# State sums moved from TensorE and PSUM to columns and accumulating DMAs, with one up and gate part issued ahead

## What is computed

```python
    x = x + jnp.tanh(g_xattn[0]) * _L0_xattn_ref(ctx_1024, _layernorm(x, axis=-1), ...)
    x = x + jnp.tanh(g_ffn[0]) * _L0_ffn_ref(_layernorm(x, axis=-1), ...)
    return x
```

```python
            def step(state, xs):
                d_t, B_t, C_t, u_t = xs
                dA = jnp.exp(d_t[..., None] * A)
                state = state * dA + (d_t * u_t)[..., None] * B_t[:, None, :]
                y_t = jnp.einsum('ben,bn->be', state, C_t)
                return (state, y_t)
            ...
            y = y + D[None, :, None] * u
            y = y * jax.nn.silu(z)
```

```python
        def _expert_ffn(x, w1, wg, w2):
            return jax.nn.silu(x @ w1) * (x @ wg) @ w2
        output = _expert_ffn(x, Ws1, Wsg, Ws2)
        ...
        for e in range(NUM_ROUTED):
            w_e = jnp.sum(topk_probas * (topk_idxs == e), axis=-1)
            output = output + _expert_ffn(x, W1[e], Wg[e], W2[e]) * w_e[..., None]
```

## Time and profile before

| | us |
|---|---|
| median of 3 runs | 1498.68 |
| lowest and highest | 1497.59, 1501.57 |
| the profiled execution | 1496.58 |
| its span, first to last instruction | 1494.5 |
| mean granted TensorE clock | 0.968 of full |
| PE busy | 1397.6 (94%) |
| DVE busy | 1053.1 (70%) |
| ACT busy | 510.0 (34%) |
| POOL busy | 453.6 (30%) |

### The profile page before, as it was taken

One profiled execution on the slowest core, in us unless ns is written; L12 is line 12 of the kernel. 1 busy time (PEld: TensorE's weight loads), 2 busy tenths in 40 slices (PEclk: granted clock), 3 DMA queues, 4 the chain that ended last, 5 costly groups with the idle time before them and its releaser, 6 DMA issues.

```text
span 1494.5 us, 18163 instructions
## 1 busy us (share of the span) xinstructions
PE 1397.6 (94%) x6311; PEld 1078.6 (72%) x6311; DVE 1053.1 (70%) x1259; ACT 510.0 (34%) x855; POOL 453.6 (30%) x240
## 2 busy tenths in 40 slices
PE   8599869999999989999999979999999999999999
PEld 4244456877777776787787867787778878888887
DVE  5898855899998974588999874689999853222222
ACT  3676625544444323432322223432332211111111
POOL 3200004687777721123323211122332211111111
PEclk9599989999999999999999999999999999999999
DMA  6111634567765574455555564455555554655552
GB/s 206 43 64 57 252 121 171 204 248 272 243 244 206 212 249 141 143 192 179 177 173 181 174 247 128 143 184 179 185 176 172 184 191 156 210 194 191 189 168 84
DMA packets 90796, 266.36 MB, mean 178 GB/s; under 512 B 11472, under 2 KB 11600, under 8 KB 90336
## 3 DMA queue, kind: packets, MB, share of 16 engines
q1 hardware_dynamic: 85472, 258.39, 51.0%
q10 hardware_dynamic: 5248, 6.96, 1.3%
HBM read 207.39 MB, written 57.93 MB: 178 GB/s over the span
## 4 chain that ended last, share of the span: by engine, by line
PE 68%; DVE 18%; issue 6%; ACT 5%; DMA 2%; SPq 1%; POOL 0%; ACTq 0%; DVEq 0%; POOLq 0%
PE ps_hg L461 19%; PE ps_h L461 18%; PE ps_y L461 12%; PE ps_y L612 7%; DVE st L1098 7%; PE ps_mid L538 5%; DVE y_rows L1104 3%; ACT dA L791 2%; PE ps_h L530 2%; DVE st L1089 1%; DVE u L1000 1%; PE ps_mid L508 1%; DVE h_tmp L1224 1%; PE ps_mid L501 1%; DVE h_tmp L1219 1%
## 5 line engine op out<-in xcount | busy, mean ns | idle before, releaser
L1363 POOL TENSOR_TENSOR h_lo<-h_tmp,h_hi 128x512 fp32r<-128x512 f32 x128 | 280.8, 2194 | 781.7 <-ACT h_hi L863 781.7
L461 PE MATMUL ps_h<-x_hi,w_split 128*128 128x512 f32 x1024 | 350.8, 404 | 9.0 <-issue 4.6
L461 PE MATMUL ps_hg<-x_hi,wg_split 128*128 128x512 f32 x1024 | 349.8, 403 | 3.4 <-DVE h_tmp L1224 3.4
L1098 DVE TENSOR_TENSOR_SCAN st<-dA,st 128x1024 f32<-128x1024 f32 x128 | 298.5, 2341 | 0.0
L461 PE MATMUL ps_y<-w_split,h_hi 128*128 128x512 f32 x1024 | 258.2, 400 | 0.8 <-ACT h_hi L863 0.8
L461 PEld LDWEIGHTS ps_h<-x_hi,w_split 128*128 128x128 f32 x1024 | 195.1, 191 | 50.8 <-issue 6.9
L863 ACT ACTIVATE h_hi<-h_tmp 128x512 fp32r<-128x512 f32 x128 | 81.0, 632 | 430.6 <-DVE h_tmp L1224 430.6
L461 PEld LDWEIGHTS ps_hg<-x_hi,wg_split 128*128 128x128 f32 x1024 | 195.3, 191 | 44.4 <-issue 4.2
L461 PEld LDWEIGHTS ps_y<-w_split,h_hi 128*128 128x128 f32 x1024 | 190.3, 190 | 40.0 <-ACT h_hi L863 2.0
L1219 DVE SCALAR_TENSOR_TENSOR h_tmp<-h_tmp,ps_h 128x512 f32<-128x512 f32 x128 | 87.8, 686 | 182.8 <-ACT h_tmp L857 182.4
L461 PE MATMUL ps_hg<-x_lo,wg_split 128*128 128x512 f32 x512 | 202.1, 395 | 0.0
(11 more groups left out here) (140 smaller groups left out, 1133.5 us busy)
## 6 DMA issues: line engine op xcount, KB each, us to landing
w_split<-split_scratch SPq DMA_DIRECT2D x192, 512.0 KB, 4.9
wg_split<-split_scratch SPq DMA_DIRECT2D x96, 512.0 KB, 4.2
split_scratch<-w_split SPq DMA_DIRECT2D x64, 512.0 KB, 4.3
b_all<-xd_scratch SPq DMA_DIRECT2D x64, 256.0 KB, 4.0
split_scratch<-wg_split SPq DMA_DIRECT2D x32, 512.0 KB, 3.1
w_raw<-in_W_dram SPq DMA_DIRECT2D x14, 1024.0 KB, 7.6
wg_raw<-in_Wg_dram SPq DMA_DIRECT2D x7, 1024.0 KB, 10.0
dA<-in_x_dram SPq DMA_DIRECT2D x4, 1024.0 KB, 11.0
```

Of the source, the lines that this page charges most:

```text
L461: mm = pe.matmul(out_, lhs[a], rhs[c], start=first and q == 0, stop=last and q == len(sides) - 1)
L1098: dve.tensor_tensor_scan(flat[1], flat[0], flat[1], 0.0, ALU.mult, ALU.add).then_inc(scan_done, 1)
L1363: pool.tensor_tensor(h_lo[:, j, :], h_tmp[j % 2][:], h_hi[:, j, :].bitcast(F32), ALU.subtract).then_inc(hl_ready, 1)
```

## The change

For batches 1 to 3 (batch 0's block alone at the start keeps its sums on TensorE):

- The state is not transposed. VectorE multiplies the scanned state by the broadcast C row in one 128x2048 instruction (`cmul`), and GpSimd issues a DMA that adds the 1 MB tile to `yacc` in SBUF (`sum_state`, which waits for `cmul` and for the previous such DMA). The last state is added by VectorE (`last_add`). The B broadcast becomes a B and C broadcast of 512 KB into `ctxT` and `in_w`, which are free by then.
- `slot` is now one quarter each of `bmul` (both halves), scan, scan, `cmul`. `bmul` of state n waits until the DMA of state n - 2 has landed, since it writes the same `st` tile.
- The `init` and `z` and `ccols` work leaves TensorE: D times u is a ScalarE copy in columns, z stays in columns. After `make_y` four groups of transposes (`y_to_rows`) bring y to rows once, and `residual` reads them from PSUM.
- `ps_hg` has two banks and `ps_y` two. TensorE's step runs up(1), gate(1) ... gate(3), then up(0) and gate(0) of the next step, then the four down tiles one at a time. VectorE, ScalarE and GpSimd follow that order.
- GpSimd's loop over the experts of batches 1 and 2 is written out.

```diff
@@ TensorE
-            def step_(step, between=lambda g: None, before_down=None):
-
+            def step_(step, ahead=True, between=lambda g: None):
+
-                for j in range(T):
+                for j in range(1, T):
                     up(step, j)
...
                     gate(step, j)
...
+                if ahead:
+                    up(step + 1, 0)
+                between(2 * T - 2)
+                if ahead:
+                    gate(step + 1, 0)
+                between(2 * T - 1)
+                for i in range(T):
+                    down(step, i)
+                    between(2 * T + i)
...
-                        front(m, *{5: ("xproj", "init0"), 6: ("dt0", "init1"), 7: ("dt1", "ccols"), 8: ("dt2", "init2"),
-                                   9: ("dt3", "init3"), 10: ("z0", "z1")}.get(g, ()))
+                        front(m, *{3: ("xproj",), 4: ("dt0",), 5: ("dt1",), 6: ("dt2",), 7: ("dt3",)}.get(g, ()))
...
-                for e in range(2, NE):
-                    step_(STEPS * b + e, state_sums(m, 3 * (e - 2)))
-                step_(STEPS * b + NE, state_sums(m, DS - 1))
+                for e in range(1, NE):
+                    step_(STEPS * b + e)
+                step_(STEPS * b + NE, False, lambda g: y_to_rows(m) if g == 5 else None)
@@ VectorE
-            def sum_rows(m, n, i):
-
-                bank, before = mid(m, sum_place(m, n, i))
-                dve.wait_ge(mid_done[bank], before + 1)
-                dve.scalar_tensor_tensor(out=y_rows[:, i, :], in0=ps_mid[bank][:], scalar=c_cols[:, i, n:n + 1],
-                                         in1=y_rows[:, i, :], op0=ALU.mult, op1=ALU.add).then_inc(mid_read[bank], 1)
+            def cmul(m, n):
+
+                odd = n % 2
+                dve.wait_ge(scan_done, 2 * (DS * m + n + 1))
+                dve.tensor_tensor(st[odd][:], st[odd][:], bc_pair[odd][:, 1:2, :].broadcast_to([P, T, L]),
+                                  ALU.mult).then_inc(cmul_done, 1)
@@ VectorE, bmul
+                    if some(m) and n >= 2:
+                        dve.wait_ge(ysum_st, sums_before(m, n - 1))
@@ GpSimd
+            def sum_state(m, n):
+
+                pool.wait_ge(cmul_done, DS * (m - 1) + n + 1)
+                if n == 0:
+                    pool.wait_ge(yinit_done, T * m)
+                if some(sums_before(m, n)):
+                    pool.wait_ge(ysum_st, sums_before(m, n))
+                pool.dma_start(yacc[:], st[n % 2][:], accum_op=ALU.add).then_inc(ysum_st, 16)
...
+                for e in range(2, NE):
+                    n = 3 * (e - 2) + 1
+                    sum_state(m, n - 1)
+                    step_(STEPS * b + e, True, lambda j: sum_state(m, n + j - 2) if j > 1 else None)
@@ ScalarE, the decays of a sum step
-                    routed_step(STEPS * b + e, lambda j: decays(m, ahead + 3 * j, ahead + 3 * (j + 1)))
+                    def some_decays(j):
+                        first = T * (3 * (e - 2) + 2) + 3 * (j - 1)
+                        decays(m, first, first + 3)
+
+                    step_(STEPS * b + e, True, lambda j: some_decays(j) if j == T else None, some_decays)
@@ SyncE
+                    sp.wait_ge(cmul_done, DS * (m - 1) + n - RING + 1)
+                src = xd_dram[m].rearrange("(c n) l -> n c l", c=2)[bass.ds(n, 1)].broadcast_to([P, 2, L])
+                sp.dma_start(bc_pair[n % RING][:], src).then_inc(bc_ld[n % RING], 16)
```

480 lines of the change are left out of this document (268 added, 212 removed).

## The result

The changed kernel takes **1520.88 us** (median of 4 runs, 1519.52 to 1523.09) against 1498.13 for the kernel before (4 runs, 1495.32 to 1501.57): a ratio of 1.0152, 95% interval [1.0127, 1.0178]. It is slower by 1.5%, where I forecast 1482; inside the range of 1452 to 1550, with the sign wrong.

A forecast was written before the change was run, and what follows sets the result against it. VectorE's work plus waits was to bound batches 1 and 2, its exclusion with GpSimd batch 0. -18 + 19.5 - 21.3 + 3 = -16.8 took 1496.58 to 1479.8, stated as 1482 us; range 1452 to 1550, the forecast's own 1466 to 1494 (0.45).

The forecast's parts named there:

- VectorE's work and waits, 38.1 a step: Sum steps of batches 1 and 2: VectorE's work of 34.1 plus waits makes 38.1 us, against 39.9; -18 in all.
- waits of 0.7, 1.9 and 1.4: VectorE, batches 1 and 2: 0.7 for up(1)'s tanh, 1.9 behind GpSimd's `h_lo`, 1.4 for a decay ahead of a tanh.
- TensorE's 32.64 hides in it, with or without the part ahead: Sum steps of batches 1 and 2: TensorE's 32.64 us of matmuls fit within VectorE's 38.1, adding nothing.
- Both at nothing while DMAs land in time.: GpSimd and SyncE queues: waits behind accumulating DMAs and fetches behind the B and C load cost nothing if DMAs land in time.
- the closest call: Accumulating DMA: taken as hidden in about 12.5 us before the waiting `bmul`; a plain 1 MB DMA lands in 11.0.
- rival 1: DMA engines bound the sum steps, an accumulate costing twice a copy: +68 us, 1550; chance 0.25.
- Rival 2: Only one accumulate's latency is too long, 12 us and 1.2 to issue: +27 us, 1509; chance 0.16.
- Batch 0, 47.5: Batch 0's sum steps: 46.9 plus 0.6 that doesn't fit, against 43.6; +19.5 us, bounds 45 and 50.6 a step.
- the exclusion: Batch 0: GpSimd instructions (20.3 us a step) and VectorE's with two SBUF inputs (26.6) can't run at once.
- my 46.9: Batch 0's sum step: GpSimd's 20.3 us and VectorE's 26.6 with two SBUF inputs, one after the other; 40.3 before.
- Front work and batch ends: Work leaving TensorE at each batch's front saves 7.1 us, -21.3 in all; batch ends cost +1 each, +3.
- Rival 4: TensorE's order ahead does nothing, having slack in every sum step; already in the forecast, with no chance of its own.

The follow-up runs named there:

- e3: Changed kernel with each accumulating DMA replaced by a plain copy of the same 1 MB, leaving out the sum over the states: 1514.4 us, one run.
- e1: Changed kernel with SyncE fetching tile 0 for the up part ahead before the load waiting for `cmul` and the down fetches: 1535.96 us, ratio 1.0268.
- e10: Changed kernel with three output banks, decays behind each tanh and SyncE's earlier tile 0 fetch, ScalarE's splits left in place: 1492.8 us, one run.
- e16: The same kernel as e10, run ten more times: 1500.0 us, ratio 1.0023 to the kernel before.
- e2: Changed kernel with each accumulating DMA cut to its first tile, 256 KB in place of 1 MB: 1518.3 us, one run.
- e12: Changed kernel with both the SyncE order of e1 and the accumulating DMA cut to its first tile: 1520.2 us, one run.
- e11: Half the change: states in columns summed by accumulating DMAs, but order, banks and list places of the kernel before: 1499.97 us, ratio 1.0017.
- e14: Kernel of e10 with `cmul` and its accumulating transfer in two 512 KB halves in batches 1 and 2: 1484.38 us, ratio 0.9914.

## Why the prediction was wrong, step by step

- **VectorE's work and waits, 38.1 a step: right as a sum, wrong as a bound.** Work 34.1 forecast, 34.3 measured; waits of 0.7, 1.9 and 1.4 forecast, 0.78, 1.64 and 1.33 measured, in the steps of e3 with nothing else in the way. That the waits agree is in part luck: the 1.64 is not GpSimd's stretching, as I had it, but twice a tanh behind three decays (1093.95 to 1095.79 us: three of L811, 1.93 us, then the tanh).
- **The step that failed** is "TensorE's 32.64 hides in it, with or without the part ahead". I followed TensorE only from a(1), where output 3 needs its bank, and got 0.7. Output 2 needs a(0) just as well, since the change took the third bank away. In the changed kernel that wait is 24.2 us in batch 0's five steps, but 5.6 in batch 1's, where the late tile 0 (21.1) comes first; with the tile early (e1) it is 28.4. Where it is long it also costs the clock, 2.3 us a step in the run with copies (38.1 to 40.4). A part's 2.72 us holds at the full clock: my sum had no term for the idle time or for the clock behind it.
- **"Both at nothing while DMAs land in time."** The fetch for up(0) was "issued some 7 us into a step, wanted at 19". It was issued that way, but stood behind four other fetches and took 14.5 us where the earlier trace rows had 11.0 for twice its size on emptier engines. That was a second chain of the same length. With the bank, the decays and SyncE's order mended together (e10, e16) the 21 us of the order ahead are back; no single one of these edits gave them.
- **The accumulating DMA, "the closest call", taken as hidden: the other step that failed.** The columns alone were forecast at 1482 and took 1500. Cutting the transfers to a quarter gives 15 us of that back in the sum steps of batches 1 and 2 (39.7 and 39.9 become 38.4 and 38.1), so the transfers were not hidden. Their price was rival 1's: 5.05 us of all engines, where the copy's was 2.5. The rule of the Trainium skill's page "Collectives: The Full Stack", section "The bandwidth ceiling: the fold count and why AG ≠ RS ≠ AR", that adding transfers run at about half the rate of copies, is stated there for rings of cores; for this DMA within one core the trace agrees with a ratio of 0.50, though its 5.05 is under the 6.4 that I made of it from the earlier trace rows. Rival 1 as a mechanism was not what held the changed kernel as a whole: e2 and e12 took the bytes away and won 1 to 3 us, no more than a single run tells. Once everything else is mended the DMA engines are full (share 1.01 at 37.2 a step), but so is VectorE. Rival 2, the landing, was real as well: 12 to 16 us against a window of 12.5, and the largest wait of VectorE in batches 1 and 2 once the lists are mended.
- **Batch 0, 47.5: the size was right for the columns alone** (47.4, e11), in part by luck: VectorE is busy 41 of it and waits for the tanh and for loads in the rest, where I had the exclusion fill it; with few bytes the steps stand at 45.7 and 46.3, under my 46.9. The Trainium skill's page "SBUF — State Buffer", section "SBUF: two separate sides", has whichever of the two starts first hold the port for the whole instruction and the other fully block. The 7.67 us scan agrees with the blocking, 5.4 over its 2.28 for four GpSimd instructions of 5.3; but its record starts 0.21 us ahead of the first of them, so the order of starting doesn't come out as stated. The 2.6 us of the changed kernel above the columns alone are what the third bank (0.9) and the decays behind the tanh (1.7) give back, one run each. ScalarE's splits are no part of it: e10 leaves them where they were and stands at 47.6.
- **Front work and batch ends:** -6.1 forecast for each of three batches. From a batch's first up part to the next one's, less the five sum steps, it was +1.9, -5.2 and -5.8. Near for two; why the first gained nothing is open.
- **Rival 4, that the order ahead does nothing,** stood in the sum at zero with no downside. It cost 21 us, more than half of the 39 between 1482 and 1521; the 18 of the columns are the rest. The order was costed by what it removes and not by the bank and the list places that it takes.

What was off is not one number but the form of the sum: I took the largest of the engines' busy times plus VectorE's waits, where the step is a round trip through VectorE, TensorE and ScalarE, and another through SyncE and the DMA engines, both 40 to 41 us long in batches 1 and 2.

## What to carry to other kernels

Count PSUM banks as a term: for each bank a change takes away, follow the round from the read that frees it to the next wait of the reader, with the matmuls behind a long idle stretch at the lower clock. When several chains have nearly one length, mending one can give nothing, or make it slower as here; mend all in one run, with the bytes taken out as well, to see the compute floor, then put them back one at a time. A transfer whose landing is waited for can be cut in halves, so that producer and consumer overlap with it: the same bytes, 1% of the kernel here, and nothing in the batch where GpSimd's list is dense.

## What the runs showed of the hardware

- An accumulating DMA between SBUF tiles holds the engines twice as long as a copy: 5.05 and 2.5 us of all sixteen for 1 MB, in runs of the same lists over the same stretch. In halves of 512 KB the queue's share was 41.4% of 197 us for 30 of them, 2.7 us each, so 5.4 for 1 MB.
- Its landing depends on what else runs: a median of 10.9 us at a DMA share of 0.90, 12.1 at 0.96, single ones of 14 to 16.
- Each costs GpSimd 0.88 us to issue, and a transfer of half the size takes as long (0.87 in e14), so halves cost twice that.
- Behind a wait for the bank, TensorE's next eight matmuls took 3.78 us after 5.00 and after 4.12 us idle (granted clock 0.50 both times), 2.75 after 2.92 (0.73), but 2.14 after 3.27 (1.00); without a wait 1.98. The length of the wait alone doesn't tell the clock behind it.
